# The order of a step's projection matmuls: bank by bank over halves of the contraction, in place of k by k

## The reference

```
y      = einsum('bct,bcd->bdt', x, cond_w[condition])      # mixing, 64 channels to 64
logits = y @ gate_w.T                                       # 8 gates
w      = softmax over the top 2 of logits, 0 elsewhere
low    = y @ lora_A.T                                       # 8 experts x rank 16 = 128 columns
out    = x + y @ base_w.T + base_b + 2 * ((low * w) @ lora_B)
```

## Time and profile before

| what | value |
|---|---|
| median of 3 runs | 493.89 us |
| profiled execution, own time | 493.61 us |
| its span, first to last instruction | 491.5 us |
| TensorE matmuls, busy | 487.4 us (99%), 2771 instructions |
| TensorE weight loads, busy | 479.2 us (97%) |
| VectorE, ScalarE, GpSimd busy | 370.8, 382.3, 129.5 us |
| granted TensorE clock | 1.000 |

### The profile page before, as it was taken

The page is one execution under the profiler, slowest core; times in us unless marked ns, Lnnn a source line. Parts: engine busy times, 40 slices in busy tenths (PEclk is TensorE's granted clock), DMA queues, the critical chain, the costliest instruction groups (busy, mean ns, idle before and its releaser), DMA issues.

```text
span 491.5 us, 8738 instructions
## 1 busy us (share of the span) xinstructions
PE 487.4 (99%) x2771; PEld 479.2 (97%) x2771; DVE 370.8 (75%) x801; ACT 382.3 (78%) x740; POOL 129.5 (26%) x111
## 2 busy tenths in 40 slices
PE   9999999999999999999999999999999999999997
PEld 8999999999999999999999999999999999999996
DVE  4977878778787778787777777787877787777654
ACT  4888778878778887778887788787788877887620
POOL 2033302333203333123332223332133320233121
PEclk9999999999999999999999999999999999999999
DMA  8812122121222231221221222212212212211112
GB/s 333 353 43 98 50 91 95 56 98 62 84 91 73 76 96 52 92 91 53 96 73 72 89 85 65 96 53 91 91 53 96 92 55 88 96 53 55 55 44 85
DMA packets 31986, 43.89 MB, mean 89 GB/s; under 512 B 18402, under 2 KB 22370, under 8 KB 31970
## 3 DMA queue, kind: packets, MB, share of 16 engines
q1 hardware_dynamic: 31826, 43.17, 25.1%
q10 hardware_dynamic: 144, 0.52, 0.4%
HBM read 25.00 MB, written 18.68 MB: 89 GB/s over the span
## 4 chain that ended last, share of the span: by engine, by line
PE 97%; ACT 2%; DVE 0%; issue 0%; POOL 0%; ACTq 0%; POOLq 0%
PE acc L654 80%; PE acc L687 9%; PE mixed L674 6%; ACT y_moved L366 1%; PE acc L783 1%; PE mixed L660 1%; ACT x_parts L353 0%; ACT w_raw L358 0%; DVE w_raw L470 0%; DVE y_turned L477 0%; ACT y_hi L389 0%; DVE w_raw L556 0%; ACT lowT_hi L381 0%; POOL zeros L273 0%; PE acc L681 0%
## 5 line engine op out<-in xcount | busy, mean ns | idle before, releaser
L654 PE MATMUL acc<-w_hi,y_hi 128*128 128x384 f32 (+3 forms) x768 | 257.3, 338 | 0.0
L654 PE MATMUL acc<-w_lo,y_hi 128*128 128x384 f32 (+3 forms) x768 | 257.0, 338 | 0.0
L654 PE MATMUL acc<-w_hi,y_lo 128*128 128x384 f32 (+3 forms) x768 | 256.7, 338 | 0.0
L366 ACT COPY y_moved<-w_raw 32x256 f32<-32x256 f32 x480 | 194.1, 404 | 37.8 <-DVE w_raw L470 32.1
L298 POOL TENSOR_TENSOR w_raw<-x_sb,bias 128x1024 f32<-128x1024 f32 x32 | 77.2, 2413 | 344.1 <-DVE low L525 258.4
L654 PEld LDWEIGHTS acc<-w_hi,y_hi 128*128 128x128 f32 x768 | 144.0, 188 | 3.8 <-ACT w_hi L339 0.2
L654 PEld LDWEIGHTS acc<-w_lo,y_hi 128*128 128x128 f32 x768 | 143.9, 188 | 2.8
L654 PEld LDWEIGHTS acc<-w_hi,y_lo 128*128 128x128 f32 x768 | 143.9, 188 | 0.6 <-DVE y_lo L455 0.3
L470 DVE TENSOR_TENSOR w_raw<-mixed,w_raw 64x1024 f32<-64x1024 f32 x60 | 73.0, 1217 | 30.2 <-ACT w_raw L358 29.8
L477 DVE STREAM_TRANSPOSE y_turned<-y_moved 128x512 f32<-128x512 f32 x60 | 42.3, 706 | 51.4 <-ACT y_moved L366 51.4
L358 ACT COPY w_raw<-mixed 64x1024 f32<-64x1024 f32 x60 | 60.9, 1015 | 21.4 <-PE mixed L674 20.6
(11 more groups left out here) (56 smaller groups left out, 238.9 us busy)
## 6 DMA issues: line engine op xcount, KB each, us to landing
x_sb<-in_x SPq DMA_DIRECT2D x32, 512.0 KB, 3.3
out<-w_raw SPq DMA_DIRECT2D x31, 512.0 KB, 2.6
w_raw<-in_proj_w SPq DMA_DIRECT2D x8, 580.0 KB, 9.5
scratch<-low_squares SPq DMA_DIRECT2D x29, 64.0 KB, 1.5
lowT_raw<-scratch SPq DMA_DIRECT2D x116, 16.0 KB, 1.7
cw<-in_cond_w ACTq DMA_DIRECT2D x1, 512.0 KB, 3.6
lb_raw<-in_lora_b SPq DMA_DIRECT2D x1, 512.0 KB, 16.3
bias<-in_base_b SPq DMA_DIRECT2D x1, 512.0 KB, 17.1
```

Of the source, the lines that this page charges most:

```text
L366: done = nc.scalar.copy(y_moved[q * SQ:(q + 1) * SQ, g, :, :], piece.rearrange("m (k q a) -> m q k a", q=QUARTERS, a=SQ)[:, q, :, :])
L654: return nc.tensor.matmul(acc[:, c % 2, b, 0:hi - lo], y_part[:, c % 2, k, :], w_part[:, k, lo:hi], start=(k == 0 and product == 0), stop= ...
```

## The change

In `step`, the loops change places. Before, k is outermost, then bank, then product. After, the eight k are cut into two halves; in a half, bank is outermost, then the half's four k, then product. The first half takes the banks 0, 1, 2, the second 2, 1, 0, so that the third bank gets its 24 matmuls one after the other. The other work is hung on a count of triples of products, 3 for each former k. The wait on `res_ready` stays ahead of the third bank's first matmul. The layout of `w_hi` and `w_lo` is as before.

```diff
-                for k in range(KT):
-                    if k % HALF_K == 0:
-                        pe.wait_ge(y_ready, 2 * s + k // HALF_K + 1)
-                    for b in range(3):
-                        if k == 0 and b == 2 and c >= 2:
+
+                threes = 0
+                for h in range(2):
+                    pe.wait_ge(y_ready, 2 * s + h + 1)
+                    for b in ((0, 1, 2) if h == 0 else (2, 1, 0)):
+                        if h == 0 and b == 2 and c >= 2:
                             pe.wait_ge(res_ready, s - 1)
-                        for product in range(3):
-                            done = project(c, k, b, product)
-
-                    if k == 0 and c == 1:
-                        mix(j, c + 1, 0)
-                    if k == (2 if c == 1 else 1) and ahead:
-                        mix(j, c + 1, 1)
-                    if k == 3 and not by_dram(c - 1):
-                        transpose_low(j, c - 1)
-                    if k == (6 if by_dram(c - 1) else 5):
...
+                        for k in range(h * HALF_K, (h + 1) * HALF_K):
+                            for product in range(3):
+                                done = project(c, k, b, product)
+                            threes += 1
+
+                            if threes == 3 and c == 1:
+                                mix(j, c + 1, 0)
+                            if threes == (9 if c == 1 else 6) and ahead:
+                                mix(j, c + 1, 1)
+                            if threes == 12 and not by_dram(c - 1):
+                                transpose_low(j, c - 1)
+                            if threes == (21 if by_dram(c - 1) else 18):
+                                if c == 1:
+                                    pe.wait_ge(lb_ready, 1)
+                                pe.wait_ge(lowT_ready, s)
+                                for bank in range(3):
+                                    last = experts(c - 1, bank)
+                                last.then_inc(lora_done, 1)
                 done.then_inc(proj_done, 1)
```

More of the change, by code:

```diff
@@ L731, in step @@
                     pe.wait_ge(banks_added, s - 1)
-                for k in range(KT):
-                    if k % HALF_K == 0:
-                        pe.wait_ge(y_ready, 2 * s + k // HALF_K + 1)
-                    for b in range(3):
-                        if k == 0 and b == 2 and c >= 2:
-                            pe.wait_ge(res_ready, s - 1)
-                        for product in range(3):
-                            done = project(c, k, b, product)
-                    if k == 0 and c == 1:
-                        mix(j, c + 1, 0)
-                    if k == (2 if c == 1 else 1) and ahead:
-                        mix(j, c + 1, 1)
-                    if k == 3 and not by_dram(c - 1):
-                        transpose_low(j, c - 1)
-                    if k == (6 if by_dram(c - 1) else 5):
[L748 to L753, removed]
+                threes = 0
```

## The result

The changed kernel takes 494.96 us (median of 21 runs, 494.64 to 495.82), the kernel before 494.06 in as many (493.74 to 494.62): ratio 1.0021, 95% interval 1.0014 to 1.0027. So it is slower, by 0.9 us, about as little as can be told.

A forecast was written before the change was run, and what follows sets the result against it. TensorE, fed back to back and busy 487.4 of 491.5 us, was taken as the bound. Terms 0 + 0 + 0 + 0 + 0.7 on the profiled execution's 493.61 us gave 494.3 us, range 492.0 to 496.4.

The forecast's parts named there:

- hooks and waits: Mixing, experts and semaphore waits in the repeated step: moved by at most 22 ns, all still covered, 0 us.
- the forecast's 14.95 to 15.01: Time in us from one step's first mixing pair to the next, expected in the after timeline if the forecast held.
- rival 2: Projection: fewer bank or address-region switches quiet the matmuls; 490.9 us if whole, twelve of one bank in 2.08 us; chance 0.22.
- rival 3: Projection: changing k every three matmuls makes them loud; up to 498.1 us, twelve of one bank in 2.12 or more; chance 0.26.
- Switches of banks at 0: Repeated step: going to another bank 4 times instead of 24 was taken to change nothing, 0 us.
- The order from the last step's rows: Projection: the last step already goes bank by bank; its spacings gave +0.3 ns on 2160 matmuls, +0.7 us.
- the third bank's +0.5 ns: Last step's 392-column matmuls: 178.8 ns each against 178.3 in the old order.
- the 384-wide +0.2: From the last step's 512-wide first bank: 1.9 ns above quietest at 384 columns, against the old order's 1.7.
- The base: Mixing pair's 230 ns, taken as the quietest 512-wide spacing, against the last step's first bank at 232.5.
- The experts and mixing at 0: Repeated step's 9 expert and 4 mixing matmuls: same operands, widths and weight loads, so 0 us.
- The slack: Some 1.6 ns per projection matmul, taken as belonging more to the matmul sequence than to other engines; not settled.
- the formula that the prediction cites: Matmul spacing of N / 2.4 + 2.5 ns, 162.5 ns for 384 columns, whatever bank or k comes next.

The follow-up runs named there:

- k_snake: Kernel before, k still outermost, banks taken 2, 1, 0 at every odd k (16 bank switches a step, not 24): 495.10 us, ratio 1.0021.
- b_pad8: Changed order with rows of the split weights 1168 columns apart in place of 1160: 494.41 us, ratio 1.0012 to the kernel before.
- alone_b: Changed order with TensorE running alone after the opening, substitute operands, output not computed: steps of 15.000 us.
- k_y32: Kernel before with an unused 128 bytes ahead of y_hi, moving y's blocks and the tensors behind them: 494.95 us, ratio 1.0017.
- k_pad56: Kernel before with rows of the split weights 1216 columns apart in place of 1160: 493.79 us, ratio 0.9995.
- b_pad56_y48: Changed order, rows 1216 columns apart, y's blocks alone moved by 192 bytes: 493.62 us, ratio 0.9993 to the kernel before.

## Why the prediction was right or wrong

- **No new wait or clock** (0 for hooks and waits): right. The list of waits is the same. The step, 15.007 us, is in the forecast's 14.95 to 15.01, and the two banks' unbroken twelves of 384 columns take 2.096 and 2.104 us, between rival 2's 2.08 and rival 3's 2.12.
- **Switches of banks at 0**: right as far as it goes. k_snake has eight fewer and is slower; with equal rows the changed order gains 0.007 us a step.
- **The order from the last step's rows, +0.3 ns on 2160 matmuls, +0.7 us**: these 72 matmuls a step measured +23 ns, +0.3 each, so the term came out as +0.7 us, and by luck. Its parts were wrong and made up for one another: the third bank's +0.5 ns was +0.9 (21 ns a step), the 384-wide +0.2 was +0.05. The base was wrong too: 230 ns was taken for the quietest 512-wide matmul, and b_pad8's mixing stands at 226.9, by which the same working would have given the 384-wide ones some +2.5 ns. And the value belongs to the rows as they lie (+0.033 us a step, +0.020 with rows 1168 apart, -0.007 with 1216), which two stretches of the last step, with other widths, could not tell.
- **The experts and mixing at 0**: this is the step that failed. With instructions and operands unchanged, I took their spacing as fixed. It was +16 and -6 ns a step, +10 together or +0.3 us over the 30 steps, a third of the whole difference. The sequence around them reaches into them.
- **The slack as belonging to the sequence and not to neighbours**: right, and shown by alone_b. The Trainium skill, "SBUF — State Buffer", section "Who interferes with whom", says that TensorE's ports are shared with no other engine; the trace agrees, 4.28 us for the third bank's run with and without the others. The same section calls TensorE's two read ports, moving operand and weight load, independent of one another. k_y32 speaks against reading that as a rule on time: the stationary blocks 128 bytes further on moved the loud group from k = 3 to k = 7. Whether the ports are where the two meet, no run shows. As to the formula that the prediction cites, the Trainium skill, "TensorE: Matmul & The Clock Gate", section "Back-to-back issue gap", gives it for an isolated matmul, not for a stream of pairs of weight load and matmul as here, and says nothing of bank or k: "by it the edit is worth exactly 0" was my reading.
- **Rival 3** (changes of k make it loud) was nearest by its sign, and its mechanism is not right: k_snake pays the same with as few changes as before. Rival 2's switch count fell with it.
- The forecast sat on the edge: 494.96 is inside the range of 492.0 to 496.4, but the ratio, 1.0021, is just past the 0.2% that I held likeliest (0.45), in the part that I had given 0.30.

Open: why four different orders with the rows as they are all come to 15.007 and the order of before to 14.973, and what in the place within 256 bytes the hardware looks at. The runs show that the place counts, not by what rule. One thing makes the agreements less strange: all fourteen step lengths, from 14.940 to 15.040 us, are whole multiples of 6.667 ns (16 cycles at 2.4 GHz) as closely as the start times tell; 14.973 is 2246 of them and 15.007 is 2251. So two sequences can agree to the ns by falling on the same multiple, as the order of before does with three different row lengths, whose groups differ. The changed order with y alone moved, rows as they are, was not run.

## What to carry to other kernels

When an engine has no waits left, a new order of the same instructions is not free and not a saving: read its spacing where the trace already has that order, over many matmuls, and expect little: here from +0.2% to -0.05% a step. In this kernel rows whose length is not a multiple of 256 bytes give each k another spacing, so an order should be compared at equal places before anything is concluded about it. And a matmul stream can be tried by itself, without the other engines, to tell own pace from traffic in one run.

## What the runs showed of the hardware

- The spacing of back-to-back fp32r matmuls, each with its weight load, is deterministic: 27 steps of 85 matmuls repeat within a ns or two, although in the same trace (before) VectorE's additions of L470 and GpSimd's of L298 shift against them by up to 0.1 and 0.3 us within twenty steps.
- The most frequent spacing of 384 columns is 173.3 ns, which is columns plus 32 cycles at 2.4 GHz, the clock that the profile shows as granted. Single ones stand up to 12 cycles below and 28 above. For 392 columns the same sum is 176.7; 177.5 (k_pad56) and 180.0 (b_pad56_y48, fifteen in a row) return more often.
- The length of a step comes in multiples of 16 cycles in all fourteen kernels.
- The spacing depends on how the moving row and the stationary block lie to each other in SBUF, modulo 256 bytes, and on the sequence before; moving the stationary blocks and what lies behind them by 128 bytes turned a step of 14.973 into 15.013 us (k_y32).
